# Attention with conditioning on one core: the sums' reduction is issued behind the first of four value chunks instead of ahead of them

## What is computed

```python
def _L0_cond_ref(x, tokens, Wq, bq, Wk, bk, Wv, bv):
    Q = _split_heads(x @ Wq.T + bq)
    K = _split_heads(x @ Wk.T + bk)
    V = _split_heads(x @ Wv.T + bv)
    tQ = _split_heads(tokens @ Wq.T + bq)
    tK = _split_heads(tokens @ Wk.T + bk)
    cQ = Q + tQ
    cK = K + tK
    scores = jnp.einsum('bhqd,bhkd->bhqk', cQ, cK) / jnp.sqrt(jnp.float32(HEAD_DIM))
    attn = jax.nn.softmax(scores, axis=-1)
    out = jnp.einsum('bhqk,bhkd->bhqd', attn, V)
    ...
x = x + _L0_cond_ref(x, cond_1024[:, None, :], ...)
```

## Time and profile before

| | |
|---|---|
| median of 3 executions | 671.43 us (671.38 to 673.34) |
| the profiled execution | 671.83 us |
| its span, first to last instruction | 670.0 us |
| TensorE busy | 661.4 us, 99% |
| VectorE busy | 538.9 us, 80% |
| GpSimd busy | 486.2 us, 73% |
| ScalarE busy | 373.4 us, 56% |

### The profile page before, as it was taken

How to read it: one execution, slowest core, us unless ns; L and a number is a source line. 1 busy time by engine, 2 the same in 40 slices (tenths; PEclk the granted TensorE clock), 3 DMA queues, 4 the chain that set the end, 5 groups by cost and what they waited for, 6 DMA issues and landing times.

```text
span 670.0 us, 10084 instructions
## 1 busy us (share of the span) xinstructions
PE 661.4 (99%) x3550; PEld 447.7 (67%) x3550; DVE 538.9 (80%) x819; ACT 373.4 (56%) x659; POOL 486.2 (73%) x202
## 2 busy tenths in 40 slices
PE   8999999999999999999999999999999999999997
PEld 6776776666776666776666676666677666675442
DVE  4676888878888878888888888887988887887886
ACT  6435565556565555565555655555555555555572
POOL 5518777788777789777779777779777778766890
PEclk9999999999999999999999999999999999999999
DMA  7943334553434554434554334554334555235401
GB/s 234 254 105 90 92 94 129 143 143 97 116 96 121 143 142 115 106 99 111 142 143 123 101 101 107 141 144 126 97 111 95 142 127 123 79 94 136 128 33 48
DMA packets 48278, 79.87 MB, mean 119 GB/s; under 512 B 9826, under 2 KB 9826, under 8 KB 48226
## 3 DMA queue, kind: packets, MB, share of 16 engines
q1 hardware_dynamic: 47700, 79.21, 44.6%
q10 hardware_dynamic: 528, 0.02, 0.0%
HBM read 19.95 MB, written 8.39 MB: 42 GB/s over the span
## 4 chain that ended last, share of the span: by engine, by line
PE 95%; DVE 2%; DMA 1%; ACT 1%; SPq 0%; issue 0%; ACTq 0%
PE bank L273 26%; PE bank L373 19%; PE bank L352 18%; PE bank L393 17%; PE bank L329 13%; DVE mf L672 1%; PE bank L401 1%; DMA Ks<-lo 1%; PE bank L424 1%; DMA cT<-condT 1%; PE bank L302 0%; ACT Pt L583 0%; DVE lo L662 0%; ACT hi L561 0%; SPq L919 0%
## 5 line engine op out<-in xcount | busy, mean ns | idle before, releaser
L583 ACT ACTIVATE Pt<-bank 128x512 f32<-128x512 f32 x512 | 299.4, 601 | 228.9 <-PE bank L373 157.3
L672 DVE TENSOR_REDUCE mf<-bank 128x1 f32<-128x512 f32 x496 | 334.1, 686 | 103.2 <-PE bank L352 102.1
L859 POOL TENSOR_TENSOR A<-A,Pt 128x2048 f32<-128x2048 f32 x59 | 270.9, 4591 | 4.6
L373 PE MATMUL bank<-Qs,Ks 98*128 98x512 f32 x496 | 201.1, 407 | 0.9 <-ACT Pt L583 0.7
L352 PE MATMUL bank<-Ks,Qs 96*128 96x512 f32 x496 | 200.4, 404 | 1.5 <-DVE mf L672 0.7
L859 POOL TENSOR_TENSOR A<-Pt 128x2048 f32<-128x2048 f32 x30 | 138.4, 4612 | 3.1 <-DVE part_sums L697 2.0
L373 PEld LDWEIGHTS bank<-Qs,Ks 98*128 98x128 f32 x496 | 93.2, 188 | 59.9 <-ACT Pt L583 39.7
L833 POOL TENSOR_TENSOR Xl<-xr,Xh 128x512 fp32r<-128x512 f32 x28 | 36.1, 1291 | 119.1 <-ACT Xh L546 119.1
L393 PE MATMUL bank<-Pt,V 128*32 128x512 f32 x1024 | 116.9, 594 | 0.0
L352 PEld LDWEIGHTS bank<-Ks,Qs 96*128 96x128 f32 x496 | 93.7, 189 | 27.5 <-DVE mf L672 5.0
L273 PE MATMUL bank<-Xl,Wh 128*128 128x512 f32 x256 | 102.6, 401 | 0.0
(11 more groups left out here) (66 smaller groups left out, 376.1 us busy)
## 6 DMA issues: line engine op xcount, KB each, us to landing
Qs<-hi SPq DMA_DIRECT2D x62, 256.0 KB, 3.6
Ks<-hi SPq DMA_DIRECT2D x62, 256.0 KB, 3.6
Qs<-lo SPq DMA_DIRECT2D x31, 256.0 KB, 4.1
Ks<-lo SPq DMA_DIRECT2D x31, 256.0 KB, 4.0
xr<-xT SPq DMA_DIRECT2D x28, 256.0 KB, 2.7
res<-xT SPq DMA_DIRECT2D x28, 256.0 KB, 2.9
outT<-ot SPq DMA_DIRECT2D x28, 256.0 KB, 3.8
Qs<-mt SPq DMA_DIRECT2D x124, 4.0 KB
```

Source lines behind the costliest of these rows:

```text
L373: e.matmul(st_bank(u)[:, :], k[0:98, j, kc * P:(kc + 1) * P], q[0:98, j, :], start=True, stop=True).then_inc(t_st, 1)
L583: e.activation(exponentials(g)[:, kc, j, :], st_bank(u)[:, :], ACT.Exp, scale=SCALE).then_inc(a_e, 1)
L672: e.reduce_max(to[:, 4 * j + qc:4 * j + qc + 1], MXB[u % 2][:, :], AXX).then_inc(v_mx, 1)
L859: e.tensor_tensor(sums, ex[:, 0, :, :] if kc == 1 else sums, ex[:, kc, :, :], ALU.add).then_inc(p_a, 1)
```

## The change

In steps 2 to 28 the totals' matmuls and their waits are issued behind the first chunk of the values instead of ahead of it. The first chunk's own waits come ahead of the totals' with it. The order of the other engines stays.

```diff
-VALUES_AT = 1
+VALUES_AT, TOTALS_BEHIND = 1, 1
...
                     if n == VALUES_AT and t >= 1:
+                        values(t - 1, range(TOTALS_BEHIND))
                         if t >= 2:
                             e.wait_ge(v_mx, u)
                             totals(t - 2, MXB[(u + 1) % 2])
-                        values(t - 1, range(KC))
+                        values(t - 1, range(TOTALS_BEHIND, KC))
...
                     if i == 0 and n == VALUES_AT:
+                        values(t - 1, range(TOTALS_BEHIND))
                         e.wait_ge(v_mx, u - 1)
                         totals(t - 2, MXB[u % 2])
-                    if n == END_VALUES_AT[i][0]:
+                        values(t - 1, range(TOTALS_BEHIND, KC))
+                    elif n == END_VALUES_AT[i][0]:
                         values(t - 1, range(KC) if len(END_VALUES_AT[i]) == 1 else (0, 1))
```

## The result

Measured 669.84 us (median of 8 executions, 668.51 to 670.76) against 671.68 us of the kernel before (8 executions): a ratio of 0.9969, 95% interval 0.9958 to 0.9981. In a later series it was 0.9966 (0.9954 to 0.9978). So the change is worth some 2 us, 0.3%. The profiled execution took 670.68 us, for a span of 668.9 us; the one before had 671.83 for 670.0.

The account below looks back on a forecast made before the run. TensorE's own instruction stream was taken as the bound; 0.09 us off each of 26 steps (2.3 us) plus 0.03 in step 2 made 2.4 us off the 671.43 median, so 669.0 us, range 668.3 to 672.3.

Parts of the forecast that it names:

- the burst in three versions: Values burst of the kernel before: 3.90 us without totals (step 1), 3.99 in step 2, 4.06 in an ordinary step.
- The head: Start of the values burst: moving the totals away takes out all 0.16 us that they cost there.
- the second wait: First values matmul behind the totals, from step 3 on: its additional wait (v_f) costs 0.04 us a step.
- The new place: Between first and second chunk of values: the totals cost 0.06 us, bounded by 0.05 and 0.16, with no wait left.
- The sum: Ordinary step 0.09 us shorter, times 26, plus 0.03 in step 2: 2.4 us off the span.
- VectorE, cost nothing: VectorE's reciprocal and what follows come 0.72 us later, using up 0.83 us of idle time; costed at nothing.
- The second cover: Behind VectorE's 0.83 us of idle time: another 0.9 us or so before a late reduction stops TensorE's matmul.
- The queues: SyncE's DMA of the keys' low part and the output store not late; ScalarE's first exponential can start 0.15 us sooner.
- only the wait is bought: Rival: totals cost 0.10 to 0.15 us at their new place, gain 0.3 to 1.6 us, about 670.6; chance 0.29.
- the bubble: Rival: within the burst three weight loads cost their full 0.11 us each, 4.6 us slower, 676.0; chance 0.08.
- a turn for each small matmul: Rival: eight small matmuls within the burst cost 0.02 us each, no gain, 0.3 us more, 671.7; chance 0.04.
- A late VectorE: Rival: VectorE's block over 0.9 us later than reckoned stops TensorE, up to about 40 us, 711; chance 0.03.

Follow-up runs that it names:

- the doubled totals: The changed kernel with each of the 27 groups of four totals matmuls issued twice in a row: 671.18 us, ratio 0.9996 to the kernel before.
- the third chunk: The changed kernel with the totals behind the third chunk of values instead of the first: 686.09 us, ratio 1.0194 to the kernel before.

## Why the prediction was right

The forecast of 669.0 us lies 0.8 below the measured 669.84, inside the range; the direction held, and "faster by over 0.3%" by the ratio of 0.9969, though its interval begins at 0.2%. Step by step:

- *TensorE's stream is the time; the burst in three versions gives the price.* Right. The whole difference of the steps is in the burst.
- *The head, 0.16 us.* Right in its sum: the burst now begins as in step 1. Of the parts, the second wait is 0.06, not 0.04: it also delays the loads within the first pass (in the kernel before, the first eight loads of values take 0.19 us in step 13, 0.16 in step 2), which the first values matmul alone did not show. The reduction's wait stays at 0.03 by subtraction; no run took it away alone. What is left, 0.06 to 0.07, is what the passes cost between chunks too.
- *The new place, 0.06 us.* Right: 0.06 in the trace, and 0.06 for each further group.
- *The sum, 0.09 a step, 2.4 us.* Right: 19.90 for 19.99 us, and 2.5 to 2.9 us between executions of like clock. The parts that the prediction could name came to 0.07, and it leaned on the whole difference of 0.10; the 0.02 between them is the second wait's missing part.
- *From the span to the time.* Here the forecast is 0.8 us off. The median that it started from was 671.43, and eight executions gave 671.68, which is 0.25 of it. The measured gain was 1.84 us instead of 2.4. Part of that can be the clock: reading "granted clock 1.00 over the steps" I left the last 40 us out, and 6 of 8 of the changed kernel's executions have 0.997, against about half of the other kernel's in later series. At about 1 us each that makes some 0.3 us; the mean clocks of the eight executions of the kernel before are not on record, and the rest is within the scatter.
- *VectorE, cost nothing.* Right, and as close as reckoned: 0.74 us later (0.72 forecast) into 0.83 of cover, with TensorE 0.09 sooner. The second cover, called 0.9, is some 1.2 us; the prediction's own rows have 308.64 − 307.43 = 1.21.
- *The queues.* Right that nothing is late for anybody, wrong in a step. "Still before its turn" was read from step 13, where the two DMAs of the high part hold SyncE for 2.01 us; in step 3 they take 1.19. So in 24 steps SyncE now waits for the low part, and its DMA is issued some 0.7 us later. That it costs nothing comes from the slack behind the DMA, which the prediction had not reckoned: luck, in this one place. ScalarE's first exponential comes 0.14 us sooner. What it waits for last there varies: GpSimd's sum 24 times and the values 4 times in the one trace, 7 and 21 times in the second.
- *The rivals.* That only the wait is bought, the bubble and a turn for each small matmul: refuted by the trace and by the doubled totals. (The small matmuls at the head start some 10 ns apart by the rows, 0.26 less 0.19 over seven, not 7; between the chunks it is 7.) A late VectorE: real as a mechanism, as the third chunk shows, but two chunks away.

## What to carry to other kernels

Work that waits, at the head of a burst that waits for nothing, costs its own wait and every wait instruction queued behind it: put it behind the first piece of ready work, and count which reader of its result becomes late and by how much. If it can't move, the order of the waits counts too: let the instruction itself carry the one that is met last (670.68 against 671.96 us here). And when a change is worth tenths of a percent, compare executions of the same mean clock, and read the windows at the end of the program as well as those of the steady steps.

## What the runs showed of the hardware that I had not expected

- Four small column-tiled matmuls in two passes cost TensorE 0.06 us between the passes of larger ones of the same tiling, their loads under the pass before; from the 128-column matmul to the 32-column ones of the values it takes 0.33 us instead of a turn of 0.24, in step 1 before and in every step of the changed kernel.
- One further semaphore wait on a matmul is an instruction of its own, of 0.05 us in step 3 of the kernel before. Long met, it costs nothing when the queue runs ahead, and 0.06 us when it stands behind a load that is still held. That a load held by a wait met early, with the late wait in an instruction of its own ahead, is slower (0.41 against 0.36 us) shows in the traces of both orders; why is open.
- TensorE's clock fell to 1.2 GHz for 3.4 us behind a stretch in which its records cover 2.50 of 2.50 us, but with loads for 1.11 us only. Busy time by records did not tell that stretch from a dense one, nor from the same stretch of the kernel before (2.70 of 2.70, loads 1.12), where the clock stayed up. Three more matmuls in it kept the clock up in 18 of 19 executions, without a shorter time to show for it; why only about half of the executions fall without them is open.
